# Convolution products of two chunks interleaved on VectorE, and a new order where the convolution passes to the qkv products

## The reference

```
# 1. token mixer (an SSM kernel), per channel h
dA    = (1 + dt*A/2) / (1 - dt*A/2)            # complex, (256, 64)
V     = dA ** l                                 # l = 0 .. 255
h     = 2 * real( (x * B) @ V )                 # (16, 256, 256) float32
# 2. h += attention block( layernorm(h) ): linear attention with 16 heads, elu + 1, then an MLP 256 -> 1024 -> 256
# 3. h += soft decision tree( layernorm(h) ): gates, 256 leaf probabilities, two matrix products
```

## Time and profile before

| what | value |
|---|---|
| median of 3 runs | 509.61 us |
| the profiled execution, its own time | 510.19 us |
| its span, first to last instruction | 508.4 us |
| TensorE matmul busy | 437.0 us, 86% |
| VectorE busy | 358.3 us, 70% |
| ScalarE busy | 291.4 us, 57% |
| GpSimd busy | 195.7 us, 38% |
| mean granted TensorE clock | 0.98 |

### The profile page before, as it was taken

How to read it: one execution, slowest core, us unless ns; L and a number is a source line. 1 busy time by engine, 2 the same in 40 slices (tenths; PEclk the granted TensorE clock), 3 DMA queues, 4 the chain that set the end, 5 groups by cost and what they waited for, 6 DMA issues and landing times.

```text
span 508.4 us, 11407 instructions
## 1 busy us (share of the span) xinstructions
PE 437.0 (86%) x3808; PEld 400.3 (79%) x3808; DVE 358.3 (70%) x867; ACT 291.4 (57%) x604; POOL 195.7 (38%) x187
## 2 busy tenths in 40 slices
PE   0048663999899999999999999999999999998974
PEld 0037663988788899888988988988988988998973
DVE  5998998995887676547476476476486586484774
ACT  3804553788876777566356457457448448446630
POOL 0496998761241210515406306306207207206020
PEclk9997997899999999999999999999999999999998
DMA  4532666344343101101002002002002001001011
GB/s 125 186 125 69 171 165 178 92 130 129 115 134 102 63 22 43 41 1 43 1 1 83 0 0 83 0 0 83 0 0 83 0 0 41 0 0 43 3 34 50
DMA packets 39871, 30.95 MB, mean 61 GB/s; under 512 B 19488, under 2 KB 35232, under 8 KB 39840
## 3 DMA queue, kind: packets, MB, share of 16 engines
q1 hardware_dynamic: 29280, 27.81, 18.0%
q10 hardware_dynamic: 10560, 2.75, 2.3%
HBM read 17.97 MB, written 12.58 MB: 60 GB/s over the span
## 4 chain that ended last, share of the span: by engine, by line
PE 71%; DVE 11%; issue 6%; ACT 4%; SPq 3%; DMA 2%; POOL 2%; DVEq 0%; ACTq 0%; POOLq 0%
PE PS L312 18%; PE PS L314 18%; PE PS L313 17%; PE PS L1476 5%; PE PS L1468 4%; PE PS L1586 3%; PE PS L1518 3%; DMA fc2raw<-in_fc2T 2%; DVE M L1048 2%; DVE Mb L1040 2%; DVE lTl L1211 1%; PE PS L1485 1%; DVE outb L1271 1%; PE PS L1538 1%; PE PS L1528 1%
## 5 line engine op out<-in xcount | busy, mean ns | idle before, releaser
L1240 DVE TENSOR_TENSOR gl<-PS,gh 128x512 fp32r<-128x512 f32 x56 | 38.7, 691 | 62.1 <-ACT gh L809 34.4
L806 ACT ACTIVATE PS<-PS,fc1bias 128x512 f32<-128x512 f32 x56 | 36.7, 655 | 75.2 <-PE PS L314 74.3
L312 PE MATMUL PS<-fc2h,gh 128*128 128x256 f32 x256 | 73.6, 288 | 2.9 <-DVE gl L1240 1.5
L538 POOL TENSOR_SCALAR pst<-mv 128x4 f32<-128x4 f32 x15 | 4.2, 282 | 185.1 <-DVE pst L1224 185.1
L314 PE MATMUL PS<-fc2l,gh 128*128 128x256 f32 x256 | 71.4, 279 | 0.0
L313 PE MATMUL PS<-fc2h,gl 128*128 128x256 f32 x256 | 71.3, 279 | 0.0
L312 PE MATMUL PS<-x2Th,fc1h 128*128 (+2 forms) x144 | 54.5, 379 | 0.0
L312 PEld LDWEIGHTS PS<-fc2h,gh 128*128 128x128 f32 x256 | 48.0, 188 | 7.0 <-DVE pst L1224 1.6
L313 PE MATMUL PS<-x2Th,fc1l 128*128 (+2 forms) x144 | 53.0, 368 | 0.0
L314 PE MATMUL PS<-x2Tl,fc1h 128*128 (+2 forms) x144 | 52.9, 367 | 0.0
L313 PEld LDWEIGHTS PS<-fc2h,gl 128*128 128x128 f32 x256 | 48.2, 188 | 1.0
(11 more groups left out here) (233 smaller groups left out, 1408.4 us busy)
## 6 DMA issues: line engine op xcount, KB each, us to landing
h<-h_scratch SPq DMA_DIRECT2D x16, 256.0 KB, 3.5
q_scratch<-qe SPq DMA_DIRECT2D x16, 256.0 KB, 2.3
qf<-q_scratch SPq DMA_DIRECT2D x16, 256.0 KB, 2.9
out_tokens<-outb SPq DMA_DIRECT2D x16, 256.0 KB, 2.2
h_scratch<-tokev ACTq DMA_DIRECT2D x10, 256.0 KB, 2.9
craw<-in_c_ri SPq DMA_DIRECT2D x16, 128.0 KB, 2.4
craw<-in_c_ri SPq DMA_DIRECT2D x32, 64.0 KB, 2.4
h_scratch<-tokev SPq DMA_DIRECT2D x6, 256.0 KB, 2.9
```

Of the source, the lines that this page charges most:

```text
L312: pe.matmul(dst, ah, bh, start=start, stop=False, **kw)
L806: act.activation(bank(j % 2), bank(j % 2), ACT.Gelu, bias=fc1bias[:, j:j + 1]).then_inc(gact, 1)
L1240: dve.tensor_tensor(gl[:, j % 2, :], bank(j % 2), gh[:, j % 2, :].bitcast(F32), ALU.subtract).then_inc(gldone, 1)
```

## The change

It has these parts. Nothing is computed otherwise, but for chunk 10, where the sum of the two products is left to TensorE.

1. X and Y get two places each: banks 2 and 3 or 4 and 5 for X, the tiles Mb and a new Mc for Y. VectorE's order in chunks 0 to 9 becomes X(n+1), sum(n), Y(n+1). The counter `vdone` counts sums alone, and `prodX` and `prodY` count the products.
2. TensorE's first products wait for five weights (`ld_w1`), no more for projT and fc2T.
3. ScalarE opens chunk 1 after it has taken the three results, since banks 4 and 5 are needed by X(1). VectorE waits for that (`staged`).
4. The four VectorE instructions from between the chunks 10 and 11 move to behind Y(2).
5. Chunk 10 has no sum: X goes straight into M, Y into Mc, and TensorE adds with twice as many matmuls (`unsummed_tokens`).
6. In chunks 10 to 12 all engines have a new order; the statistics of step s come one step later (`STATS`, `norm1_stats(s + 3)`), and GpSimd waits for less.

The diff, cut to its core:

```diff
-STATS = {5: (8,), 6: (9,), 7: (10, 11), 8: (12,), 9: (13,), 10: (14,), 11: (15,)}
+STATS = {4: (7,), 5: (8,), 6: (9,), 7: (10, 11), 8: (12,), 9: (13,), 10: (14,), 11: (15,)}
...
+        Mc = sb("Mc", [P, CH, NA, EX])
...
+        def added(n):
+            return n + 1 - (n >= SINGLE)
...
+            for dst, src in ((wqraw, wq), (leafraw, leafT), (woutraw, woutT), (fc1raw, fc1T)):
+                load_weight(dst[:, :, :], src, ld_w1)
+            for dst, src in ((projraw, projT), (fc2raw, fc2T)):
+                load_weight(dst[:, :, :], src, ld_w2)
...
             scales(0)
-            pool.wait_ge(xh1, CREDIT + 4)
+            pool.wait_ge(xh1, CREDIT + 2)
             rotate(FIRST // 2, 0)
             scales(1)
             scales(2)
+            pool.wait_ge(xh1, CREDIT + 4 * 2 + 2)
             for n in range(FIRST, CHUNKS - 1):
...
             def tables(n):
-                act.wait_ge(vdone, CREDIT + 3 * n - 4 + (3 if n > SINGLE else 0))
+                act.wait_ge(prodY, CREDIT + (n if n > SINGLE else n - 1))
...
             def paired_tables(it, par):
                 n = 2 * it + par
-                act.wait_ge(vdone, CREDIT + 3 * n - 4)
+                act.wait_ge(prodY, CREDIT + n - 1)
...
-            for par in range(2):
-                opened(0, par)
+            opened(0, 0)
             act.wait_ge(pe_set, 3)
...
+            opened(0, 1)
...
             operands(SINGLE)
+            tables(SINGLE + 1)
             closed(SINGLE // 2 - 1, 1)
             operands(SINGLE + 1)
-            tables(SINGLE + 1)
-            for n in range(SINGLE + 1, CHUNKS):
+            token_row(SINGLE)
+            tables(SINGLE + 2)
+            operands(SINGLE + 2)
+            y_high(0)
+            for n in range(FIRST, CHUNKS):
                 s = n - FIRST
                 token_row(n - 1)
-                y_high(s + 1)
+                if s > 0:
+                    y_high(s + 1)
                 q_parts(s)
...
                 kv_parts(s, 0)
+                if s == 0:
+                    y_high(s + 1)
                 kv_parts(s, 1)
...
+            def overlapped(n, par):
+                first_product(n + 1, 1 - par)
+                product_sums(n, par)
+                second_product(n + 1, 1 - par)
+
+            first_product(0, 0)
+            second_product(0, 0)
+            dve.wait_ge(staged, 2)
+            overlapped(0, 0)
+            overlapped(1, 1)
+            dve.wait_ge(act_set, 1)
+            tt(qkvl[:, :, :], qkvraw[:, :, :], qkvh[:, :, :].bitcast(F32), ALU.subtract)
...
+            tt(fc1bias[:, :], fc1bias[:, :], b1add[:, :], ALU.add)
+            dve.wait_ge(pool_set, POOL_TABLES + 6)
...
+            link(dve.tensor_copy(vt[:, :, :, P], one.to_broadcast([P, 2, KD])))
+            link(dve.tensor_copy(vt0[:, :, :, P], one.to_broadcast([P, B, KD])))
+            with dve.Fori(1, 3) as it:
+                for par in range(2):
+                    overlapped(2 * it + par, par)
+            for n in range(6, SINGLE - 1):
+                overlapped(n, n % 2)
+            product_sums(SINGLE - 1, 1)
...
-            products(SINGLE, 7)
-            product_sums(SINGLE, SINGLE % 2)
+            unsummed_products(SINGLE)
+            single_product(SINGLE + 1, 0)
+            single_product(SINGLE + 1, 1)
             norm1_stats(0)
-            link(dve.tensor_copy(vt[:, :, :, P], one.to_broadcast([P, 2, KD])))
-            link(dve.tensor_copy(vt0[:, :, :, P], one.to_broadcast([P, B, KD])))
...
-            tt(qkvl[:, :, :], qkvraw[:, :, :], qkvh[:, :, :].bitcast(F32), ALU.subtract)
...
-            tt(fc1bias[:, :], fc1bias[:, :], b1add[:, :], ALU.add)
+            single_sums(SINGLE + 1)
             norm1_apply(0)
             norm1_stats(1)
-            products(SINGLE + 1, 7)
-            product_sums(SINGLE + 1, 1)
             norm1_stats(2)
             y_low(0)
-            norm1_stats(3)
-            norm1_apply(1)
             for n in range(FIRST, CHUNKS):
                 s = n - FIRST
-                products(n, 7)
-                product_sums(n, n % 2)
-                y_low(s + 1)
+                single_product(n, 0)
+                single_product(n, 1)
+                if s == 0:
+                    norm1_apply(1)
+                    norm1_apply(2)
+                single_sums(n)
+                if s > 0:
+                    y_low(s + 1)
                 q_elu(s)
-                norm1_apply(s + 2)
-                if s + 4 < GROUPS:
-                    norm1_stats(s + 4)
-                k_elu(s, 0)
+                if s > 0:
+                    norm1_apply(s + 2)
+                else:
+                    k_elu(s, 0)
+                    y_low(s + 1)
+                norm1_stats(s + 3)
+                if s > 0:
+                    k_elu(s, 0)
                 k_elu(s, 1)
...
+            def unsummed_tokens(n):
...
+                pe.wait_ge(prodX, CREDIT + n + 1)
+                pe.wait_ge(prodY, CREDIT + n + 1)
+                pe.wait_ge(tokout, CREDIT + n - 1)
+                for i in range(CH):
+                    rows = slice(64 * (i % 2), 64 * (i % 2) + 64)
+                    dst = PS[rows, 0, (i // 2) * SH:(i // 2 + 1) * SH]
+                    shifted = dst.rearrange("p (a e) -> p a e", a=NA)[:, :, 1:NE]
+                    for x, w in enumerate((Wa, Wb)):
+                        c = w[:, n % 2, i, :, :].rearrange("p c d -> p (c d)")
+                        pe.matmul(dst, c, M[:, n % 2, i, :, :].rearrange("p a e -> p (a e)"), start=x == 0, stop=False,
+                                  skip_group_check=True)
+                        mm = pe.matmul(shifted, c, Mc[:, i, :, :], start=False, stop=x == 1, skip_group_check=True)
...
-            pe.wait_ge(ld_w2, 16 * 7)
+            pe.wait_ge(ld_w1, 16 * 5)
...
+            unsummed_tokens(SINGLE)
+            y_transposes(0)
+            tokens(SINGLE + 1, 1, None)
+            pe.wait_ge(dve_set, DVE_ALL)
+            for n in range(FIRST, CHUNKS):
+                s = n - FIRST
+                if s > 0:
+                    y_transposes(s + 1)
+                q_products(s)
+                kv_products(s, 0)
+                if s == 0:
+                    y_transposes(s + 1)
+                kv_products(s, 1)
+                tokens(n, n % 2, None)
```

More of the change, by code:

```diff
@@ L157, in vit_tower @@
         qraw_at = cursor[0]
+        cursor[0] = tables_at + size([P, 2, KD, HT])
+        Mc = sb("Mc", [P, CH, NA, EX])
+        assert cursor[0] <= qraw_at
+        cursor[0] = qraw_at
         qe = sb("qe", [P, 2, KD, HT])
@@ L363, in store_q, with load_weight @@
                 sp.dma_start(qs[:, :, s % GROUPS, x].rearrange("k p x -> p k x"), qe[:, s % 2, :, :]).then_inc(qst[s % 2], 16)
-            def load_weight(dst, src):
-                sp.dma_start(dst, src.rearrange("(k p) o -> p k o", p=P)).then_inc(ld_w2, 16)
+            def load_weight(dst, src, done):
+                sp.dma_start(dst, src.rearrange("(k p) o -> p k o", p=P)).then_inc(done, 16)
             for par in range(2):
@@ L370, in _ @@
             sp.wait_ge(pool_set, 1)
[L371 to L374, removed]
+            load_weight(routraw[:, :, 0:LEAVES - 1], routersT, ld_w1)
+            for dst, src in ((wqraw, wq), (leafraw, leafT), (woutraw, woutT), (fc1raw, fc1T)):
+                load_weight(dst[:, :, :], src, ld_w1)
+            for dst, src in ((projraw, projT), (fc2raw, fc2T)):
+                load_weight(dst[:, :, :], src, ld_w2)
             for n in range(2, FIRST):
@@ L1029, in _ @@
             assert count[0] == DVE_U, count[0]
-            def products(n, b):
-                dve.wait_ge(xyld, CREDIT + n + 1)
[L1033 to L1040, removed]
+            Ma = [PS[:, b:b + 2, :].rearrange("p b x -> p (b x)")[:, 0:CH * NA * EX].rearrange(
+                "p (h a e) -> p h a e", h=CH, a=NA) for b in (2, 4)]
@@ new lines, in product, with first_product @@
+            def product(n, b, r, to):
+                xy = PS[:, b, 0:D].rearrange("p (h x a) -> p h x a", h=CH, x=2)
+                x = xy[:, :, r, :].unsqueeze(3).to_broadcast([P, CH, NA, EX])
+                w = (Er, Ei)[r][:, bass.ds(n * CH, CH), :].unsqueeze(2).to_broadcast([P, CH, NA, EX])
+                dve.tensor_tensor(to, x, w, ALU.mult).then_inc((prodX, prodY)[r], 1)
+            def first_product(n, par):
+                dve.wait_ge(xyld, CREDIT + n + 1)
+                dve.wait_ge(vdone, CREDIT + n - 1)
+                product(n, 7 - par, 0, Ma[par])
@@ L1042, in product_sums, with second_product @@
+            def second_product(n, par):
+                dve.wait_ge(vdone, CREDIT + n - 1)
+                product(n, 7 - par, 1, (Mb, Mc)[par][:, :, :, :])
             def product_sums(n, par):
                 dve.wait_ge(tokmm, CREDIT + n - 1)
[L1045 to L1048, removed]
@@ L1050, in _ @@
-            dve.wait_ge(pool_set, POOL_TABLES)
-            with dve.Fori(0, PAIRS // 2) as it:
```

(23 more changed lines are left out.)

47 lines of the change are left out of this document (22 added, 25 removed).

## The result

The changed kernel takes 515.40 us (4 runs, 514.22 to 516.98), the kernel before beside it 509.27. The ratio is 1.011, 95% interval 1.009 to 1.013. The forecast was 507.2, with a range that ended at 511.3. The profiled execution of the changed kernel took 516.03 us.

The account below looks back on a forecast made before the run. It took TensorE to bound the kernel from 100 us on, VectorE to pace the loop before. Tokens 12 coming earlier gave 510.19 - 2.45 = 507.7 us for the profiled execution, 507.2 against the median, range 504.5 to 511.3.

Parts of the forecast that it names:

- The four moved instructions: Behind Y(2) on VectorE: they take about 3.0 us as in the old place, so tokens 2 start at 52.85.
- Five weights, start: At the kernel's start: waiting for five weights gains nothing by itself; tokens 0 start at 43.7, where it was 43.43.
- One loss of clock (B): Rival, chance 0.25: a 3.15 us TensorE gap before tokens 2 drops the clock, costing 1.6 us; 508.8 us in all.
- the circle: In the loop: tokens, ScalarE's result copy and table, product and sum wait on each other, 7.16 us per two chunks.
- Interleaving: In the loop: the new VectorE order gives 3.58 us per chunk, where it was 3.36, so the loop gets slower.
- Chunk 10 without a sum: At chunk 10: removes 1.09 us of VectorE, adds 4.26 us of TensorE, hidden with 1.2 us to spare.
- The passage: From the loop to the qkv pass: tokens 12 start at 93.9, where it was 96.35, a gain of 2.45 us.
- VectorE keeps the same work ... No gain, no loss: In the stretch behind the passage: VectorE had 18.09 of 20 us and keeps the same work, so nothing changes.
- Its own sign of being wrong: The prediction is wrong if the loop keeps 3.36 us or if tokens 12 don't come before 95.
- Rival C: Rival, chance 0.15: uneven gaps make the clock fall repeatedly in the loop, three falls costing 4.8 us; 512.0 us.

Follow-up runs that it names:

- e1: The changed kernel with the four moved VectorE instructions one chunk earlier, behind Y(1) instead of Y(2), where GpSimd is idle; 511.35 us, 1.003 of the kernel before.
- e12: The changed kernel with the two copies of ones in the moved block replaced by memsets of 1.0; 513.14 us, 1.006 of the kernel before.
- e2: The changed kernel with ScalarE's loop tables one chunk ahead, chunk n+3's table ahead of chunk n's result; 513.17 us, 1.007 of the kernel before.
- e6: The changed kernel with the interleaving alone undone from chunk 3 to chunk 8, both places for each product kept; 510.83 us, 1.002 of the kernel before.
- e9: The changed kernel with qkv statistics at their old step and GpSimd's rotations 14 and 15 held until VectorE's preceding kvm ends; 515.59 us, 1.010 of the kernel before.
- e13: The changed kernel with both copies of ones as memsets and seven unread matmuls between tokens 1 and tokens 2; 512.44 us, 1.004 of the kernel before.
- e3: The changed kernel with the statistics of the qkv pass back at their old, earlier step; 516.37 us, 1.014 of the kernel before.
- e8: The changed kernel with 13 matmuls of constants, whose result nothing reads, added on TensorE ahead of tokens 2; 515.0 us, 1.008 of the kernel before.

## Why the prediction was wrong

The step that failed is "The four moved instructions take the VectorE time that they had, about 3.0 us". They took 6.6, with the idle time behind them, because GpSimd rotates beside them in their new place. The prediction saw the meeting and looked at one side of it: it let `qkvl` stretch the rotations and never asked what the rotations do to the three short instructions. In the old place three of the four stood where no rotation ran, and the one copy that met the end of a rotation took 0.81 us; the earlier trace rows skip it, and the 3.0 us took it in as if it were work. e1 (the four take 2.4 us) and e12 (two of them 0.15) show it.

Point by point:

- *Five weights, start*: right. Tokens 0 start at 43.85 (43.7).
- *The four moved instructions*: wrong by 3.6 us. Tokens 2 come at 56.47 (52.85).
- *One loss of clock (B)*: happened. Tokens 2 took 3.67 us. The longer gap, 6.00 us and not 3.15, belongs to the failed step. Its price of 1.6 us was about right: tokens 4 follow tokens 2 by 8.71 us, where the circle alone would be 7.16. Tokens 8 start 22.7 us after tokens 2 (21.5 forecast without the loss).
- *Interleaving*: right in mechanism and size, 6.97 for 7.16; e2 removes the circle as the argument says. But the comparison was short. It set 3.58 against the 3.36 of before and took the interleaving and the second places for one thing; e6 shows that the places alone give 3.22 and that the order takes this away again.
- *Chunk 10 without a sum*: hidden, as forecast. It ends at 89.51, before the transposes at 90.00, though with 0.5 us to spare and not 1.2; it took 4.85 us and not 4.26.
- *The passage*: right, 17.6 us for 17.4.
- *"VectorE keeps the same work ... No gain, no loss"*: wrong by 1.7 us. The work is the same; its neighbours on GpSimd are not. That it is the mechanism of the block is shown by e9 for the two later steps (0.4 us); for the first step (1.3 us) it is read from the trace, where `qe` and `kvm` are 1.8 us longer in all, and no run tests it.
- *The clock near the end*: 1.5 us in the profiled execution, in no case of the prediction.
- *Its own sign of being wrong*: tokens 12 not before 95. They came at 98.81.

At tokens 12 it is 4.9 us: 3.6 by the block, 1.2 by the lost clock less the slightly faster circle, 0.1 by the passage. Together with 1.7 and 1.5 that is 8.1 of the 8.3 between 507.7 and 516.03. Rival C, slower at 512.0, was not the cause: between 60 and 81 the changed kernel showed no second fall, though e9, e12 and e13 had one there.

## What to carry to other kernels

When an instruction moves, list what the engine beside it does at the new place, and ask in both directions which of the two is held. In this kernel a short VectorE instruction with two inputs in SBUF, or a short copy from SBUF to SBUF, cost what was left of the GpSimd instruction that it met, so place it where GpSimd idles, or write a constant instead of copying it. And two places for a buffer are one change, issuing the next product early is another: the early product brings its own waits ahead of the sum that the next engine needs, so try the places alone. And what a fast loop gains must still pass the next stage: e1 and e2 lost about 2 us of it again while they waited for data there.

## What the runs showed of the hardware

Beside a GpSimd `tensor_tensor` of 128x768 (1.6 us) these were held to its end: `fc1bias` of 8 columns, two SBUF inputs (0.17 to 1.35 us); copies from SBUF to SBUF of 4 and 32 columns (0.17 to 1.50, 0.20 to 1.44); `qe` and `kvm` (0.69 to 1.21, 0.4 to 1.73). Not held were memsets (0.06, 0.09), products and sums with one input in PSUM (1.08 to 1.10 everywhere) and statistics (0.75 at 90.00, beside a rotation that began at 90.15). The hold goes both ways: beside `qkvl` (1.75 us) a rotation took 2.89. Where GpSimd's instructions follow each other, the turns mostly alternated (1.35, 1.50, 1.44 us; two `kvm` of e3, one rotation each, 3.32 together), but in e8 one copy missed three turns: 4.46 us.

The Trainium skill states the rule (SBUF — State Buffer, Who interferes with whom): the pair of ports that VectorE shares with GpSimd is an exclusive lock, held for the whole instruction; a VectorE instruction with two SBUF inputs contends with a GpSimd instruction that reads SBUF, and one with at most one SBUF input, outside the modes that use both ports, does not. By that rule `fc1bias`, `qe` and `kvm` are held, and products, sums, statistics and memsets pass, as measured. The two copies have one SBUF input, so by it they are held only if they run in a mode that uses both ports; they were held (1.50 and 1.44 us), but no run shows in which mode they ran.
